# Requeuing the transfers of pre-summed weights and the next chunk's tokens in a gated WKV + FFN block, and moving chunk 0's low parts of activations from GpSimd to VectorE

## The chip, the cores and the metric

The kernel runs on one core of a Trainium2 chip. The metric is the device time of one execution in microseconds (us). The engines are TensorE (PE, matmuls; PEld is its weight load), VectorE (DVE), ScalarE (ACT) and GpSimd (POOL). SyncE (SP) computes nothing here: it waits on semaphores and issues most DMAs, so its program is called the SP queue below. POOL issues the DMAs that add while they copy.

## The reference, cut to what matters

```python
# x, ctx: (16, 256, 512) float32
x = x + tanh(g_xattn) * wkv(time_decay, time_first, k=layernorm(x), v=ctx)   # a scan over the 256 tokens
h = silu(layernorm(x) @ W1.T) * (layernorm(x) @ W3.T)                        # 512 -> 2048
x = x + tanh(g_ffn) * (fwht(h) @ W2.T)                                       # Hadamard transform, 2048 -> 512
```

## The kernel before

The 4096 tokens are cut into 8 chunks of 512 tokens (two batches each). The Hadamard transform is folded into W2 at the start. Each float32 matmul operand is split into a float16 high part and a bfloat16 low part, and three matmuls (high by high, high by low, low by high) replace one.

**Weights.** W1 and W3 come in 16 units (two units make a piece of 256 hidden channels, so there are 8 pieces). `unit_hi` (ACT) and `unit_lo` (DVE) split a unit in place; the semaphore `raw_lo` counts the units that are ready. `put_plain(p)` on SP stores a finished piece to the DRAM scratch `up_stage`, for use by the later chunks.

**Sums.** Chunks 1 to 7 use a block scheme with fewer products, which needs sums of weight blocks. POOL forms these in DRAM (`up_sums`) for four groups of two pieces, each in four steps of two DMAs: `copy_group`, then the accumulating DMAs `add_first`, `add_second` and `add_third`. Before each step POOL waits until the step before it of the same group has landed. `load_again(n)` on SP brings the sums of unit n into one of three buffers, after `add_third` of its group has landed and (from n = 3 on) after buffer n - 3 was used. `weight_parts(n)` on DVE splits them (lines 1451 and 1454) into one of two output buffers, and `put_sums(n)` on SP stores that to `up_stage`. `weight_parts(n)` waits for the load, and from n = 2 on also for the store `put_sums(n - 2)`. `load_pair` fetches one piece, plain and sums, for the block scheme.

**Stages.** Run 0 and Run 1 are the two halves of chunk 0. After a preamble, `ffn(Run(1))` works through 16 hidden tiles j. For each tile PE makes a gate product (`pg`), a linear product (`pl`), and the down product of tile j - 2; ACT takes the silu of the gate (L964), DVE multiplies (`times_lin`, L1398) and rounds to float16 (`hidden_hi`, L1405), and POOL subtracts the high part from the product (`hidden_lo`, L1683). Between those, in an order written out by hand in `FIRST_AT`, the engines prepare chunk 1 (called Run 2 in the code): token moments `tok`, scans `scan_b` and `scan_a` (L1267) with a scaling of each on ACT (L899), `over`, the residual, the mean and the variance (PE matmuls L607 and L612 in PE's own order), normalising. `next_tok` takes the token moments of the chunk after that (Run 3), whose tokens `load_tokens(2)` brings into `bv` (L1211 reads them). `unit_slot` says at which tile ACT and DVE split the units 8 to 15, and `SUMS_AT` at which tile DVE does which `weight_parts`. From `pairs(Run(2))` on, chunks 1 to 7 go through the block scheme in eight pairs of tiles each (lines 714 to 737).

**Order.** Every engine and the SP queue work in program order; semaphores tie them. PE must have all 16 units (`raw_lo` 16) before tile 14. In the preamble POOL also clamps 16 tiles of W2 (`tile_clamp`, L1688); PE's `less_hi(i)` (L636) waits for the clamp of tile i.

```python
def hidden_lo(run, j):                       # on POOL
    pool.wait_ge(hid_hi, run.tile(j))
    pool.tensor_tensor(hl[...], hf[...], hh[...], ALU.subtract).then_inc(hid_lo, 1)
...
def load_x(c):                               # on SP; load_tokens(c) follows it with no wait of its own
    sp.wait_ge(x1_done, c * NB)
```

Of the kernel before, what the change touches and what calls it, by code (L numbers as in the profile page):

```python
# [21 lines left out]
SLOTS = H // P  # L22
# [39 lines left out]
                num=8, inv=8, over=9, resid=9, mean=(11, 1), centre=10, square=11,  # L62
                sum_var=11, var=(13, 0), rsqrt=13, norm=14, next_tok=11)

SUMS_AT = {4: (0,), 5: (1,), 7: (2,), 8: (3,), 10: (4,), 11: (5,), 12: (6,), 13: (7,)}
LATE_SUMS = {0: (8,), 1: (9,), 2: (10,), 3: (11,), 4: (12, 13), 5: (14, 15)}
# [3 lines left out]
GROUPS = ((0, 2), (2, 4), (4, 6), (6, 8))  # L70

STEPS_AT = {0: ((0, "second"),), 1: ((1, "first"),), 2: ((0, "third"),), 3: ((2, "copy"),), 4: ((1, "second"),),
            5: ((1, "third"),), 6: ((2, "first"),), 7: ((3, "copy"),), 8: ((2, "second"),), 9: ((2, "third"),),
            10: ((3, "first"),), 11: ((3, "second"),), 12: ((3, "third"),)}


def flamingo_block(nc, xt_in, x_in, v_in, w1_in, w3_in, w2_in, mats_in, stage, up_sums, factor_rows, out):
    with ExitStack() as ctx:
# [224 lines left out]

        unit_slot = {0: (8, 9), 1: (10, 11), 3: (12,), 4: (13,), 12: (14, 15)}
        places = (0, 1, 2, 3, 4, 5, 0, 1, 6, 7, 8, 9, 10, 11, 12, 13)
# [66 lines left out]
        def _(sp):  # L372
# [39 lines left out]
            def put_plain(p):  # L412

                sp.wait_ge(raw_lo, 2 * p + 2)
                sp.dma_start(stage[p][:, 0, :], piece(p)).then_inc(plain_put[p], 16)
# [101 lines left out]
            load_unit(15)  # L517
            put_plain(3)
            for n in range(0, 3):
                load_again(n)  # L520
            put_plain(4)
            put_plain(5)
            put_sums(0)
            load_again(3)
            put_sums(1)
            put_plain(6)
            load_again(4)
            put_sums(2)
            load_again(5)
            put_sums(3)  # L530
            load_again(6)
            load_v(2)
            put_sums(4)
            load_again(7)
            load_x(2)
            load_tokens(2)
            put_sums(5)
            put_plain(7)
            put_factors(Run(3))
# [639 lines left out]
        def _(dve):  # L1179
# [228 lines left out]
            def hidden_tile(run, j):  # L1408
                times_lin(run, j)
                hidden_hi(run, j)  # L1410

            def channel_sum(run, which):

# [43 lines left out]
            def ffn(run):  # L1457

                ahead = Run(2, 1)
                for j in range(SLOTS):  # L1460
# [18 lines left out]
                    if j == SLOTS - 1:  # L1479
                        plain_lo(ahead, 0)  # L1480
                        sums_lo(ahead, 0)
                    hidden_tile(run, j)
                    if at(j, "resid"):
                        residual(ahead, 0)
                        residual(ahead, 1)
                        channel_sum(ahead, 0)
# [172 lines left out]
        def _(pool):  # L1659
# [70 lines left out]
            def ffn():  # L1730

                for j in range(SLOTS):
                    hidden_lo(Run(1), j)
                    for g, step in STEPS_AT.get(j, ()):
                        if step == "copy":
                            copy_group(g)
                        if step == "first":
                            add_first(g)
                        if step == "second":
                            add_second(g)  # L1740
                        if step == "third":
                            add_third(g)

# [27 lines left out]
            copy_group(0)  # L1771
            for i in range(3, 11):
                tile_clamp(i)
            pool.wait_ge(rows_mm, 2 * KT)
            for j in range(0, 2):
                hidden_lo(Run(0), j)
            add_first(0)
            copy_group(1)
            for i in range(11, 13):
# [3 lines left out]
            for i in range(13, TILES):  # L1783
                tile_clamp(i)
            ffn()
            pairs(Run(2, 1, 0))
# [54 lines left out]
```

## Time and profile before

| | |
|---|---|
| median of 3 runs | 1056.58 us (1054.04 to 1057.97) |
| the profiled execution | 1057.62 us, of which the span of its instructions is 1055.8 us |
| PE busy | 997.6 us, 94% of the span |
| DVE busy | 801.8 us, 76% |
| ACT, POOL busy | 439.6 us, 274.2 us |
| mean granted TensorE clock | 0.988 of full speed |

The profiled execution lies 1.0 us above the median. Its span is what the traces below are measured in. PE is busy for nearly all of it, so time is lost where PE has gaps or runs at the lower clock level, and the chain that ended last runs on PE for 69% of the span.

### The profile page before, as it was taken

The numbers are of one execution on the slowest core, as the hardware profiler recorded it, in microseconds if no ns is written. First come the engines' busy times: TensorE is split into PE (matmuls) and PEld (weight loads), VectorE is DVE, ScalarE is ACT, GpSimd is POOL, SyncE is SP. The second block draws the span as 40 slices with busy tenths as digits, with TensorE's granted clock in tenths as the row PEclk, the third lists the DMA queues.
The fourth block names the chain that finished last, engine by engine and source line by source line (L and its number), as shares of the span: only waits on it lengthen the run. The fifth ranks groups of instructions, "written<-read, shape, count | busy, mean of one in ns | idle before, by whom it ended". The sixth has DMA issues, their size and how long they took to land.

```text
span 1055.8 us, 17503 instructions
## 1 busy us (share of the span) xinstructions
PE 997.6 (94%) x6988; PEld 691.6 (66%) x6988; DVE 801.8 (76%) x1288; ACT 439.6 (42%) x736; POOL 274.2 (26%) x212
## 2 busy tenths in 40 slices
PE   5799899689999999999999999999999999999998
PEld 4565344256677677776777777777777777777775
DVE  7977594989989995889769995889669994753334
ACT  6875342246243443455243542444243542522221
POOL 1344232211432033211422124221322124211111
PEclk9999999799999999999999999999999999999999
DMA  9699999694885446354745446353645433444331
GB/s 352 233 340 291 321 255 227 109 355 168 293 301 173 151 188 240 100 213 155 267 164 178 146 177 239 114 218 143 264 160 180 163 126 151 160 166 165 125 145 41
DMA packets 47042, 210.03 MB, mean 199 GB/s; under 512 B 9328, under 2 KB 26864, under 8 KB 36336
## 3 DMA queue, kind: packets, MB, share of 16 engines
q1 hardware_dynamic: 38128, 192.13, 50.2%
q0 software_dynamic: 8832, 16.78, 7.6%
q8 instruction: 55, 0.90, 0.3%
q14 instruction: 27, 0.22, 0.1%
HBM read 183.70 MB, written 41.97 MB: 214 GB/s over the span
## 4 chain that ended last, share of the span: by engine, by line
PE 69%; DVE 17%; DMA 6%; issue 5%; ACT 2%; SPq 0%; DVEq 0%; POOL 0%
PE pl L714 8%; PE pl L716 8%; PE pl L715 8%; PE po L726 7%; PE po L728 7%; PE pg L714 6%; PE pg L715 6%; PE pg L716 6%; PE po L737 4%; PE po L735 4%; DMA bv<-x_tok 2%; DMA wts<-up_stage 2%; DVE x L1432 2%; DVE work L1604 2%; DVE bv L1295 1%
## 5 line engine op out<-in xcount | busy, mean ns | idle before, releaser
L1759 POOL TENSOR_TENSOR work<-work 128x512 bf16<-128x512 f32 x112 | 163.9, 1464 | 595.4 <-DVE work L1604 595.4
L726 PE MATMUL po<-work,w 128*128 128x512 f16 x456 | 173.0, 379 | 2.2 <-DVE x L1432 1.3
L728 PE MATMUL po<-work,w 128*128 128x512 f16 x456 | 172.8, 379 | 0.0
L1060 ACT ACTIVATE work<-work 128x256 f32<-128x256 f32 x168 | 68.4, 415 | 210.2 <-DVE work L1511 210.1
L714 PE MATMUL pg<-wts 128*128 128x256 f16 x448 | 122.5, 273 | 4.8 <-DVE work L1511 4.7
L1511 DVE TENSOR_TENSOR work<-pl,wts 128x256 f32<-128x256 f32 x168 | 65.1, 414 | 80.1 <-PE pl L716 77.5
L715 PE MATMUL pg<-wts 128*128 128x256 bf16 x448 | 122.4, 273 | 0.0
L716 PE MATMUL pg<-wts 128*128 128x256 f16 x448 | 122.4, 273 | 0.0
L714 PE MATMUL pl<-xn,wts 128*128 128x256 f16 x448 | 122.3, 273 | 0.0
L715 PE MATMUL pl<-xn,wts 128*128 128x256 bf16 x448 | 122.2, 273 | 0.0
L716 PE MATMUL pl<-xn,wts 128*128 128x256 f16 x448 | 122.1, 273 | 0.0
L716 PE MATMUL pl<-wts 128*128 128x256 f16 x448 | 122.1, 273 | 0.0
L715 PE MATMUL pl<-wts 128*128 128x256 bf16 x448 | 122.1, 273 | 0.0
L714 PE MATMUL pl<-wts 128*128 128x256 f16 x448 | 122.1, 273 | 0.0
L1604 DVE TENSOR_SCALAR work<-work 128x512 f16<-128x512 f32 x112 | 91.3, 815 | 8.2 <-PE po L737 0.5
L735 PE MATMUL po<-work,w 128*128 128x512 bf16 x228 | 86.4, 379 | 0.0
L737 PE MATMUL po<-work,w 128*128 128x512 bf16 x228 | 86.4, 379 | 0.0
L1034 ACT COPY wts<-pg 128x512 f32<-128x512 f32 x56 | 32.6, 582 | 123.9 <-PE pg L716 123.9
L726 PEld LDWEIGHTS po<-work,w 128*128 128x128 f16 x456 | 44.6, 98 | 52.7 <-DVE x L1432 9.6
L728 PEld LDWEIGHTS po<-work,w 128*128 128x128 bf16 x456 | 44.6, 98 | 39.4
L714 PE MATMUL pg<-xn,wts 128*128 128x256 f16 x224 | 61.3, 274 | 4.9 <-DMA wts<-up_stage 3.6
L1511 DVE TENSOR_TENSOR work<-pg,early 128x256 f32<-128x256 f32 x56 | 23.6, 421 | 55.6 <-PE pg L716 54.8
(206 smaller groups left out, 2159.6 us busy)
## 6 DMA issues: line engine op xcount, KB each, us to landing
wts<-up_stage SPq DMA_DIRECT2D x56, 2048.0 KB, 8.0
up_stage<-wts SPq DMA_DIRECT2D x8, 1024.0 KB, 13.2
up_stage<-wts SPq DMA_DIRECT2D x16, 512.0 KB, 8.2
ev<-ctx_t SPq DMA_DIRECT2D x7, 1024.0 KB, 11.0
xin<-x_t SPq DMA_DIRECT2D x7, 1024.0 KB, 7.5
bv<-x_tok SPq DMA_DIRECT2D x7, 1024.0 KB, 10.0
out_t<-x SPq DMA_DIRECT2D x7, 1024.0 KB, 4.8
wts<-up_sums SPq DMA_DIRECT2D x11, 512.0 KB, 9.0
```

Source lines behind the costliest of these rows:

```text
L714: pe.matmul(bank, hi, ah, start=(start and k == 0), stop=False, skip_group_check=True)
L715: pe.matmul(bank, hi, al, start=False, stop=False, skip_group_check=True)
L716: mm = pe.matmul(bank, lo, ah, start=False, stop=(stop and k == 1), skip_group_check=True)
L726: pe.matmul(po[:, d, :], w2h[:, j, d * P:d * P + P], hh[:, b, :], start=start, stop=False, skip_group_check=True)
L728: pe.matmul(po[:, d, :], w2l[:, j, d * P:d * P + P], hh[:, b, :], start=False, stop=False, skip_group_check=True)
L735: pe.matmul(po[:, d, :], w2h[:, j + 1, d * P:d * P + P], hl[:, b + 1, :], start=False, stop=False, skip_group_check=True)
L737: pe.matmul(po[:, d, :], w2h[:, j, d * P:d * P + P], hl[:, b, :], start=False, stop=((p - 1) % PAIRS == PAIRS - 1), skip_group_check=True) ...
L1034: act.copy(early1[:, w, :], chain_fifth[w]).then_inc(kept1, 1)
L1060: act.activation(sg[:, slot, cols], src, ACT.Silu, scale=(1.0, -1.0)[slot]).then_inc(acted, 1)
L1511: dve.tensor_tensor((sg, hf)[w][:, slot, b * T:b * T + T], bank, other, ALU.add).then_inc(joined, 1)
L1604: dve.tensor_scalar(hh[:, 2 * (p % 2) + slot, :], hf[:, slot, :], F16_MAX, -F16_MAX, ALU.min, ALU.max).then_inc(pair_hi, 1)
L1759: pool.tensor_tensor(hl[:, b, :], hf[:, slot, :], hh[:, b, :], ALU.subtract).then_inc(pair_lo, 1)
```

## The change

`add_first(0)`, `copy_group(1)`, `add_second(0)`, `add_first(1)` and `add_third(0)` are issued earlier in POOL's preamble, and POOL's part of `ffn` is only the remaining DMA steps, with no `hidden_lo` between them. `hidden_lo` of Run 1's sixteen tiles is done by DVE right behind `hidden_hi`. Units 14 and 15 are split at tiles 4 and 5 (they were split at 12), `next_tok` goes from tile 11 to 12, the `weight_parts` are placed anew, and the SP queue is reordered.

```diff
-                sum_var=11, var=(13, 0), rsqrt=13, norm=14, next_tok=11)
-SUMS_AT = {4: (0,), 5: (1,), 7: (2,), 8: (3,), 10: (4,), 11: (5,), 12: (6,), 13: (7,)}
+                sum_var=11, var=(13, 0), rsqrt=13, norm=14, next_tok=12)
+SUMS_AT = {5: (0, 1), 8: (2,), 10: (3, 4), 11: (5,), 13: (6,), 14: (7,)}
...
-        unit_slot = {0: (8, 9), 1: (10, 11), 3: (12,), 4: (13,), 12: (14, 15)}
+        unit_slot = {0: (8, 9), 1: (10, 11), 3: (12,), 4: (13, 14), 5: (15,)}
...
             put_plain(3)
+            put_plain(4)
+            put_plain(5)
             for n in range(0, 3):
                 load_again(n)
-            put_plain(4)
-            put_plain(5)
+            put_plain(6)
             put_sums(0)
             load_again(3)
             put_sums(1)
-            put_plain(6)
             load_again(4)
+            put_plain(7)
+            load_v(2)
             put_sums(2)
             load_again(5)
+            load_x(2)
+            load_tokens(2)
             put_sums(3)
             load_again(6)
-            load_v(2)
             put_sums(4)
             load_again(7)
-            load_x(2)
-            load_tokens(2)
             put_sums(5)
-            put_plain(7)
...
+            def hidden_lo(run, j):                 # on DVE
+                if j == 0:
+                    dve.wait_ge(hid_lo, Run(0).tile(AHEAD - 1))
+                if j >= HBUF:
+                    dve.wait_ge(down, run.down(j - HBUF))
+                dve.wait_ge(hid_hi, run.tile(j))
+                dve.tensor_tensor(hl[...], hf[...], hh[...], ALU.subtract).then_inc(hid_lo, 1)
...
             def ffn():                             # on POOL
-                for j in range(SLOTS):
-                    hidden_lo(Run(1), j)
-                    for g, step in STEPS_AT.get(j, ()): ...
+                add_second(1)
+                for g in range(2, len(GROUPS)):
+                    copy_group(g)
+                    add_third(g - 1)
+                    add_first(g)
+                    add_second(g)
+                add_third(len(GROUPS) - 1)
```

DVE's order from tile 4's product on, before (L1438 and L1441 split a unit, L1451 and L1454 are a `weight_parts`):

```order
L1398 TENSOR_TENSOR work<-work,pl 128x512
L1405 TENSOR_SCALAR work<-work 128x512
L1438 TENSOR_SCALAR wts<-wts 128x1024
L1441 TENSOR_TENSOR wts<-x,wts 128x1024
L1451 TENSOR_SCALAR wts<-wts 128x1024
L1454 TENSOR_TENSOR wts<-wts 128x1024
L1398 TENSOR_TENSOR work<-work,pl 128x512
L1405 TENSOR_SCALAR work<-work 128x512
L1451 TENSOR_SCALAR wts<-wts 128x1024
L1454 TENSOR_TENSOR wts<-wts 128x1024
```

The same stretch of DVE in the changed kernel (L1394, L1401 and L1415 are the product, its high part and its low part; L1444 and L1447 a unit, L1457 and L1460 a `weight_parts`):

```order
L1394 TENSOR_TENSOR work<-work,pl 128x512
L1401 TENSOR_SCALAR work<-work 128x512
L1415 TENSOR_TENSOR work<-work 128x512
L1444 TENSOR_SCALAR wts<-wts 128x1024
L1447 TENSOR_TENSOR wts<-x,wts 128x1024
L1444 TENSOR_SCALAR wts<-wts 128x1024
L1447 TENSOR_TENSOR wts<-xn,wts 128x1024
L1394 TENSOR_TENSOR work<-work,pl 128x512
L1401 TENSOR_SCALAR work<-work 128x512
L1415 TENSOR_TENSOR work<-work 128x512
L1444 TENSOR_SCALAR wts<-wts 128x1024
L1447 TENSOR_TENSOR wts<-xn,wts 128x1024
```

The low part is new behind each high part; units 14 and 15 (the rows that read `xn`) now stand at tiles 4 and 5, ahead of the first two `weight_parts`, which both follow at tile 5.

POOL's preamble before, from its fourth W2 clamp on (L1711 is `add_first`, L1700 `copy_group`, L1683 `hidden_lo`, L1688 a clamp, L1720 `add_second`):

```order
L1688 TENSOR_SCALAR w<-w 128x4x128 [waits w2_hi] x8
L1683 TENSOR_TENSOR work<-work 128x256 [waits hid_hi,rows_mm]
L1683 TENSOR_TENSOR work<-work 128x256 [waits hid_hi]
L1711 DMA up_sums<-w_t 512x1x256 [waits summed0_0]
L1711 DMA up_sums<-w_t 512x1x256 [waits summed0_1]
L1700 DMA up_sums<-w_t 16x16384 x2
L1688 TENSOR_SCALAR w<-w 128x4x128 [waits w2_hi] x2
```

The same place in the changed kernel (L1718 is `add_first`, L1707 `copy_group`, L1695 a clamp, L1690 `hidden_lo`, L1727 `add_second`):

```order
L1695 TENSOR_SCALAR w<-w 128x4x128 [waits w2_hi] x5
L1718 DMA up_sums<-w_t 512x1x256 [waits summed0_0]
L1718 DMA up_sums<-w_t 512x1x256 [waits summed0_1]
L1707 DMA up_sums<-w_t 16x16384 x2
L1695 TENSOR_SCALAR w<-w 128x4x128 [waits w2_hi] x3
...
L1727 DMA up_sums<-up_sums 256x256 [waits summed0_0]
L1727 DMA up_sums<-up_sums 256x256 [waits summed0_1]
L1718 DMA up_sums<-w_t 512x1x256 [waits summed1_0]
L1718 DMA up_sums<-w_t 512x1x256 [waits summed1_1]
L1695 TENSOR_SCALAR w<-w 128x4x128 [waits w2_hi] x2
```

The clamps of W2's tiles 11 and 12 (the last row of each) now stand behind two steps that wait for DMAs to land, `add_second(0)` and `add_first(1)`.

## Rows read from the trace of the kernel before

**Rows 1.** The page, busy time of each engine over the span.

```profile
PE 997.6 (94%) x6988; PEld 691.6 (66%) x6988; DVE 801.8 (76%) x1288; ACT 439.6 (42%) x736; POOL 274.2 (26%) x212
```

**Rows 2.** Busy time by stretch: stretch, length, PE, PEld, DVE, ACT, POOL, PEclk, DMA share, GB/s.

```profile
125.90:131.20 5.30, 0.12 (x1) 0.02 (x1) 3.61 (x4) 3.16 (x6) 1.95 (x3) 0.91 1.01 311
131.20:139.20 8.00, 7.99 (x24) 3.01 (x25) 7.86 (x7) 4.86 (x5) 2.35 (x3) 0.64 1.02 176
139.20:147.10 7.90, 7.90 (x37) 3.45 (x36) 7.76 (x6) 7.74 (x8) 4.34 (x6) 1.00 0.84 270
195.20:212.50 17.30, 17.29 (x72) 7.34 (x72) 16.75 (x20) 8.56 (x10) 2.62 (x2) 0.91 1.06 176
400.00:1055.80 655.80, 647.19 (x4783) 467.28 (x4780) 466.96 (x778) 250.66 (x446) 161.92 (x110) 1.00 0.46 168
```

**Rows 3.** Waits of PE from 73 to 217 us: total, times, longest.

```profile
PE pg L645 <- DVE wts L1441: 12.5, 1, 12.5
PE pg L645 <- ACT work L964: 6.1, 2, 5.2
PE pg L714 <- DMA wts<-up_stage: 3.6, 1, 3.6
```

**Rows 4.** DVE in order of time, 90 to 216 us: start, duration, instruction, idle time before.

```profile
98.84 0.69 DVE L1398 TENSOR_TENSOR work<-work,pl 128x512 f32<-128x512 f32 x1 [3.11 <-PE pl L647]
...
115.32 0.69 DVE L1451 TENSOR_SCALAR wts<-wts 128x1024 f16<-128x1024 f32 x1 [12.83 <-DMA wts<-up_sums]
116.05 1.23 DVE L1454 TENSOR_TENSOR wts<-wts 128x1024 bf16<-128x1024 f32 x1
...
119.04 2.06 DVE L1454 TENSOR_TENSOR wts<-wts 128x1024 bf16<-128x1024 f32 x1
...
121.22 2.37 DVE L1254 TENSOR_TENSOR ev<-ev 128x1028 f32<-128x1028 f32 x2
123.51 4.48 DVE L1267 TENSOR_TENSOR_SCAN eb<-decays,ev 128x1028 f32<-128x1028 f32 x2
...
163.73 2.35 DVE L1337 TENSOR_TENSOR eb<-x,pst 128x1024 f32<-128x1024 f32 x2 [2.15 <-PE pst L607]
...
184.71 2.47 DVE L1211 BATCH_NORM_STATS2 parts<-bv 128x6 f32<-128x512 f32 x4 [11.07 <-DMA bv<-x_tok]
...
212.62 0.68 DVE L1398 TENSOR_TENSOR work<-work,pl 128x512 f32<-128x512 f32 x1
```

**Rows 5.** One group of DVE's high parts, 78.8 to 213.4 us: busy, mean ns.

```profile
L1405 DVE TENSOR_SCALAR work<-work 128x512 f16<-128x512 f32 x11 | 4.7, 427 | 1.2
```

**Rows 6.** PE in order of time: a `less_hi`, and the end of tile 5's linear product.

```profile
69.96 0.38 PE L636 MATMUL po<-w,minus 128*128 128x512 f16 x1
...
107.29 0.38 PE L653 MATMUL po<-work,w 128*128 128x512 f16 x1
```

**Rows 7.** ACT in order of time: the scaling behind `scan_b`.

```profile
128.03 2.56 ACT L899 ACTIVATE ev<-ev,cc 128x512 f32<-128x512 f32 x4 [14.33 <-DVE eb L1267]
```

**Rows 8.** The SP queue in order of time: when it issued its DMAs.

```profile
106.31 2.59 SPq L426 DMA_DIRECT2D wts<-up_sums  x2
...
169.55 0.61 SPq L406 DMA_DIRECT2D bv<-x_tok  x1
...
196.22 0.97 SPq L447 DMA_DIRECT2D wts<-up_stage  x1
```

**Rows 9.** POOL in order of time: `add_first(0)`, clamps 11 and 12, `add_third(0)`, a `hidden_lo`.

```profile
59.43 2.75 POOL L1711 DMA_DIRECT2D up_sums<-w_t  x2
...
67.85 1.32 POOL L1688 TENSOR_SCALAR w<-w 128x512 f16<-128x512 f16 x2 [4.65 <-ACT w L983]
...
93.94 0.87 POOL L1727 DMA_DIRECT2D up_sums<-up_sums  x1
...
118.55 1.47 POOL L1683 TENSOR_TENSOR work<-work 128x512 bf16<-128x512 f32 x1 [14.08 <-DVE work L1405]
```

**Rows 10.** Issue to landing: POOL's four DMAs of 59 to 61.5 us; `put_sums(3)`.

```profile
DMA to landing us min/median/max: 13.0/19.4/23.4
...
up_stage<-wts SPq DMA_DIRECT2D x1, 512.0 KB, 7.9
```

More of the change, by code:

```diff
@@ L70 @@
 GROUPS = ((0, 2), (2, 4), (4, 6), (6, 8))
-STEPS_AT = {0: ((0, "second"),), 1: ((1, "first"),), 2: ((0, "third"),), 3: ((2, "copy"),), 4: ((1, "second"),),
-            5: ((1, "third"),), 6: ((2, "first"),), 7: ((3, "copy"),), 8: ((2, "second"),), 9: ((2, "third"),),
-            10: ((3, "first"),), 11: ((3, "second"),), 12: ((3, "third"),)}
 def flamingo_block(nc, xt_in, x_in, v_in, w1_in, w3_in, w2_in, mats_in, stage, up_sums, factor_rows, out):
@@ L1410, in hidden_tile @@
                 hidden_hi(run, j)
+            def hidden_lo(run, j):
[4 more added lines that the diff above has]
+                dve.wait_ge(hid_hi, run.tile(j))
+                dve.tensor_tensor(hl[:, j % HBUF, run.cols(j)], hf[:, j % 2, run.cols(j)],
+                                  hh[:, j % HBUF, run.cols(j)], ALU.subtract).then_inc(hid_lo, 1)
             def channel_sum(run, which):
@@ L1482, in ffn @@
                     hidden_tile(run, j)
+                    hidden_lo(run, j)
                     if at(j, "resid"):
@@ L1730, in ffn @@
             def ffn():
-                for j in range(SLOTS):
-                    hidden_lo(Run(1), j)
[L1734 to L1742, printed above, removed]
+                add_second(1)
[5 more added lines that the diff above has]
+                add_third(len(GROUPS) - 1)
             def pairs(run, front=True):
@@ L1771, in _ @@
             copy_group(0)
-            for i in range(3, 11):
+            for i in range(3, 8):
+                tile_clamp(i)
+            add_first(0)
+            copy_group(1)
+            for i in range(8, 11):
                 tile_clamp(i)
@@ L1776, in _ @@
                 hidden_lo(Run(0), j)
-            add_first(0)
-            copy_group(1)
+            add_second(0)
+            add_first(1)
             for i in range(11, 13):
@@ L1784, in _ @@
                 tile_clamp(i)
+            add_third(0)
             ffn()
```

## The prediction

> **What bounds the kernel now.** First the page: PE is busy 94% of the span [rows 1]. Then busy time by stretch: from 400 us to the end PE works 647.2 of 655.8 us at full clock [rows 2], and the change touches nothing there. So the gain or loss must come from the first 220 us, the part in which chunk 0 runs and the weights are prepared. There I read the waits of PE [rows 3]: 12.5 us for the last unit of W1/W3 ahead of tile 14, 5.2 us for one silu ahead of tile 8 (the 6.1 us of the row is this one and a short one), 3.6 us for the first `load_pair`. The stretches show what a gap costs beside itself: after the 5.2 us gap the clock is 0.64 for 8 us, in which PE does 24 matmuls; at full clock it does 37 in 7.9 us, so 24 take 5.1 us and 2.9 us are lost to the 1.2 GHz level. After the 12.5 us gap the 72 matmuls of 195.2 to 212.5 take 17.3 us where they should take 15.4, so 1.9 us are lost [rows 2]. PE's recoverable time is 5.2 + 2.9 + 12.5 + 1.9 = 22.5 us; the 3.6 us gap stands apart.
>
> Third, what is late behind those waits, on DVE [rows 4]. DVE sat idle 12.8 us until 115.3 for the first sums, because `load_again(0)` was issued at 106.3 [rows 8], after `add_third(0)`, which POOL issued at 93.9 behind a `hidden_lo` [rows 9]. Everything behind it in DVE's order slid: `scan_b` started at 123.5, ACT's scaling waited for it until 128.0 [rows 7], the silu of tile 7 stands behind that on ACT, and PE needed it. Later DVE idled 11.1 us until 184.7 for chunk 2's tokens, issued at 169.55 [rows 4, 8], and the units 14 and 15 stood behind that wait.
>
> **The change part by part.** I walk DVE's order, the queue that decides, and check PE against it.
>
> Low parts on DVE. A 128x512 operation of two inputs takes 0.69 us, the high part 0.43 us [rows 4, 5]. The trace has no such subtraction on DVE. Bounds: 0.43 from below; from above 1.23, the cost of twice the elements [rows 4]. I take 0.7, the same shape and kind. Twelve full tiles and four half ones add 12 x 0.7 + 4 x 0.4 = 10 us. Against it stands a saving. `weight_parts` L1454 takes 1.23 us alone, but 2.06 at 119.04, while POOL's `hidden_lo` ran from 118.55 [rows 4, 9]. I count nine such DVE operations beside a `hidden_lo`, so 9 x 0.83 = 7.5 us go away. Net cost some 2.5 us over the stage; without the saving 10 us, with the low bound below zero.
> The Trainium skill, "SBUF — State Buffer", section "Who interferes with whom", says that a DVE instruction with two SBUF inputs contends with a GpSimd instruction that reads SBUF, and that the later one blocks wholly. By that rule the 119.04 one waits until 118.55 + 1.47 = 120.02 and ends at 121.25, 2.21 us; the row says 2.06. The rule would put the saving at up to 9 x 0.98 = 8.8 us and the net at 1.2 us; nothing below uses that.
>
> First sums. POOL can issue `add_third(0)` once clamps and `add_second(0)` are through, which I put at 77 to 81 us, not 93.9: `add_second(0)` now goes out near 63 and lands some 14 us later. The load goes out 12.4 us behind (106.3 - 93.9), at 90 to 94, and lands 9 us behind that (115.3 - 106.3), plus up to 3 us for the two plain stores now ahead of it: 102 to 106. DVE: tile 4 at 98.8 as before, + 1.8 for product, high and low part, + 2 x 1.65 for units 13 and 14 (each 0.42 + 1.23) = 103.9. Tile 5's linear product ends near 107.4 [rows 6]; + 1.9 and unit 15 gives 111.0, and only there are the sums wanted, so no wait. Two `weight_parts` at 1.9: 114.7. Weighing 2.4 and scan 4.5 end at 121.6; before, 128.0. `scan_b` is 6.4 us earlier, and the silu of tile 7 comes at 124.6 + 0.6, before PE wants it (125.9). PE's first gap and its clock loss, 8.1 us, go. The silu of tile 8, behind ACT's second scaling, only gains 6.4 us: PE waits about 1.6 us there instead. PE at the mean's matmul is 8.1 - 1.6 = 6.5 us earlier.
>
> Tiles 7 to 11. `weight_parts(3)` leaves tile 8 for tile 10, so DVE reaches its wait for the mean 7 us earlier and still waits: mean at 163.7 - 6.5 = 157.2. From there before took 9.9 us to the end of the second channel sum (163.7 to 184.7 - 11.1 = 173.6). Now `weight_parts(3)` adds 1.9, a low part 0.7, less 0.8 of POOL's disturbance: 157.2 + 11.7 = 168.9.
> A new wait stands in it. `weight_parts(5)` needs the store `put_sums(3)`, which cannot go out before `weight_parts(3)` at 161.5, four us before it is wanted (165.3). Before, that store had been out since tile 8. With its 7.9 us [rows 10] it lands at 169.4: 4 us of waiting, end at 173. Bounds: nothing if it lands in 3.8 us; 11 us if it takes the 15.1 us that the tokens took (184.7 - 169.55), since they are queued just ahead of it. Behind the wait stand the channel sum, PE's variance matmul and so the linear product of tile 13: PE loses some 3 us there.
>
> Tiles 12 to 15. The tokens are issued behind the residual at 151.5 and land by 167, wanted at 175: the 11.1 us wait goes. Units 14 and 15 are long done, so the 12.5 us gap and its 1.9 us go. DVE from the start of the token moments to the end of tile 15's product took 213.3 - 184.7 = 28.6 us. Less tile 12's product (1.1) and the two units (4.0), less 1.5 of disturbance, plus two low parts 1.4, plus 0.7 for the reciprocal root on ACT: 24.1. So 173 + 1.9 (tile 12) + 24.1 = 199. The block scheme cannot start before tile 15's product. PE itself would be through tile 13's down product at 212.5 - 22.5 + 1.6 + 3 to 5 = 195 to 197. DVE is the bound, at 199; the wait there replaces the 3.6 us one. `load_pair(0)` goes out at 181 (before 196.2, landing 19.8 us later), so it lands at 201 at the worst, 192 when less is queued.
>
> W2's clamps. Clamps 11 and 12 ran at 67.85, and `less_hi(11)` at 69.96 [rows 6, 9], a slack of 1.4 us. They now stand behind `add_first(1)`, which waits for `copy_group(1)`. POOL issues `add_first(0)` and that copy at 46 to 51 instead of 59.4. Then they took 13.0 to 23.4 us [rows 10], and from 59.4 the last was in at 84.7. The same from 46.2 gives 71.5, the clamp at 73.5 and 4.3 us of delay for PE; with the low end 13 us after 51, nothing. I take 2 us. This delay moves everything behind it.
>
> Sum: the block scheme starts at 199 + 2 = 201 instead of 216.1. Gain 15 us, on the span 1055.8 - 15 = 1041. The profiled run is 1.0 above the median, so 1056.6 - 15 = **1041.5 us**. Chunk 1's remaining work keeps its distance to PE: DVE ends its preparation 2.8 us behind PE's start, where before it began `scale` 2.5 us behind.
>
> **The rivals.**
> 1. *Better than that (0.16).* The store is quick and the copy lands in time: 4 + 2 us more, gain 21, 1035.5 us. For it: DMA engines are less loaded once the plain stores are early. Against it: tokens and `load_x(2)` are 2 MB just ahead of the store.
> 2. *DVE's new chain eats more (0.18).* The sums or the store land late (11 us instead of 4), or the low part costs 1.2 us. Gain 3 to 9, 1048 to 1053. For it: DVE is busy nearly throughout from 110 to 170 us.
> 3. *Slower (0.06).* POOL now waits for its DMAs with PE's clamps behind. Lost is every microsecond by which `copy_group(1)` lands after 67, and it decides from a landing at 67 + 17 = 84 us, 34 us after issue, against 23.4 as the longest seen. At 40 us it would be 1063.
> A page rule bears on this one: the Trainium skill, same page, "A bandwidth-pool intuition that's wrong", says that POOL's DMAs wait for descriptors while DVE runs some two-port operations. By that rule the chain on POOL would be late by DVE operations of 0.4 to 1.2 us each (an estimate from rows), not by tens; I see DMA issues of 2.75 us for two [rows 9] and give it no more weight.
> 4. *No change (0.05).* The gaps only move to the end of the stage.
>
> **How the numbers follow.** The forecast (gain 10 to 18, 1038.5 to 1046.5) has 0.55. The 80% range takes in rival 1 and most of rival 2: 1034 to 1052. A measurement of this kernel can tell about 0.5%, 5.3 us, from no change. Faster: 0.55 + 0.16 + two thirds of rival 2 = 0.84; slower 0.05; same 0.11.
>
> **What would show it.** Right: DVE's 12.8 and 11.1 us waits gone; PE's 12.5 us wait for L1441 gone; L1454 at 1.23 us throughout; block scheme starting near 201. The new waits to look for: `weight_parts(5)` for an `up_stage` store, PE for the variance's channel sum, PE ahead of `less_hi(11)` for a POOL clamp, PE at pair 0 for DVE. Wrong if the first sums still land after 111, or if PE stands still before 74 us.

## The result, and the profile after

| | before | changed |
|---|---|---|
| median | 1056.58 us (1054.04 to 1059.15, 9 runs) | 1049.68 us (1047.17 to 1052.58, 9 runs) |
| ratio | | 0.9937, 95% interval 0.9921 to 0.9952 |
| the profiled execution: span | 1055.8 us | 1047.9 us |
| start of the block scheme | 216.1 us | 206.9 us |

The changed kernel is 6.9 us faster. I had forecast 15. It was measured once more among the experiments below, again beside the kernel before: 9.7 us faster, ratio 0.9904 [0.9887, 0.992]. The two intervals just miss each other, so differences of 0.3% between ratios that were taken apart say little below.

The page of the changed kernel, busy time:

```profile
PE 992.5 (95%) x6922; PEld 692.4 (66%) x6988; DVE 802.5 (77%) x1304; ACT 439.9 (42%) x736; POOL 254.5 (24%) x196
```

PE's work is what it was (some of its records are missing here, 6922 of 6988), so the difference is again one of gaps and of the clock. In the numbering of the changed kernel `less_hi` is L632, the gate product L641, the silu L960, `times_lin` L1394, `hidden_lo` L1415, `weight_parts` L1457 and L1460, the clamp L1695, `add_first` L1718, `copy_group` L1707, `add_second` L1727, `add_third` L1734 and the block scheme starts at L710.

Waits of PE after, from 40 to 330 us: total, times, longest.

```profile
PE po L632 <- POOL w L1695: 9.5, 1, 9.5
PE pg L641 <- ACT work L960: 3.8, 4, 1.9
PE pg L710 <- DVE work L1394: 3.4, 1, 3.4
```

Against [rows 3]: the 12.5 us wait for the units is gone, the waits for the silu are short ones, and the wait at the block scheme is for DVE instead of for `load_pair`. All that was forecast. The first line was forecast too, but at 2 us: PE stands still 9.5 us for a clamp of W2, nearly as long as what was removed (6.9 us when the changed kernel was profiled again).

PE in order of time, and the stretch behind that gap (PE, PEld, DVE, ACT, POOL, PEclk, DMA share, GB/s):

```profile
79.78 0.61 PE L632 MATMUL po<-w,minus 128*128 128x512 f16 x1 [9.47 <-POOL w L1695]
...
206.93 0.37 PE L710 MATMUL pg<-xn,wts 128*128 128x256 f16 x1 [3.44 <-DVE work L1394]
```

```profile
79.00:84.30 5.30, 4.52 (x15) 3.17 (x16) 1.38 (x2) 2.83 (x5) 2.60 (x6) 0.65 1.17 257
```

The `less_hi` that ran at 69.96 [rows 6] now runs at 79.78, and behind the gap the granted clock is 0.65, the 1.2 GHz level for most of the stretch. POOL tells why, in order of time:

```profile
46.28 2.83 POOL L1718 DMA_DIRECT2D up_sums<-w_t  x2
47.62 2.51 POOL L1707 DMA_DIRECT2D up_sums<-w_t  x2
...
62.06 0.92 POOL L1727 DMA_DIRECT2D up_sums<-up_sums  x1 [2.40 <-DMA up_sums<-w_t]
72.14 0.91 POOL L1727 DMA_DIRECT2D up_sums<-up_sums  x1 [9.15 <-DMA up_sums<-w_t]
74.73 1.30 POOL L1718 DMA_DIRECT2D up_sums<-w_t  x1 [1.69 <-DMA up_sums<-w_t]
77.76 1.30 POOL L1718 DMA_DIRECT2D up_sums<-w_t  x1 [1.73 <-DMA up_sums<-w_t]
78.42 1.87 POOL L1695 TENSOR_SCALAR w<-w 128x512 f16<-128x512 f16 x2
...
86.51 1.87 POOL L1734 DMA_DIRECT2D up_sums<-up_sums  x2
```

Issue to landing of the two `add_first(0)` DMAs of 46.3 and 47.0 us:

```profile
DMA to landing us min/median/max: 15.5/20.2/24.9
```

Clamps 11 and 12 ran at 67.85 before [rows 9] and run at 78.42 now. Ahead of them in POOL's order stand `add_second(0)`, which waits for `add_first(0)` to land, and `add_first(1)`, which waits for `copy_group(1)`. The second DMA of `add_first(0)` took 24.9 us, to 71.9. The two copies, issued at 47.6 and 48.1, took 26.8 and 29.3 us, to 74.4 and 77.4, and held the next two issues until 74.7 and 77.8. The landing of the last copy is thus what the clamps were waiting for in the end.

DVE after, in order of time, answering to [rows 4]:

```profile
110.38 0.69 DVE L1394 TENSOR_TENSOR work<-work,pl 128x512 f32<-128x512 f32 x1 [2.43 <-PE pl L643]
111.70 0.69 DVE L1415 TENSOR_TENSOR work<-work 128x512 bf16<-128x512 f32 x1
...
122.55 0.69 DVE L1457 TENSOR_SCALAR wts<-wts 128x1024 f16<-128x1024 f32 x1
123.27 1.23 DVE L1460 TENSOR_TENSOR wts<-wts 128x1024 bf16<-128x1024 f32 x1
...
128.77 4.48 DVE L1263 TENSOR_TENSOR_SCAN eb<-decays,ev 128x1028 f32<-128x1028 f32 x2
...
169.00 2.35 DVE L1333 TENSOR_TENSOR eb<-x,pst 128x1024 f32<-128x1024 f32 x2 [2.52 <-PE pst L603]
...
176.92 0.69 DVE L1457 TENSOR_SCALAR wts<-spare 128x1024 f16<-128x1024 f32 x1
...
182.58 2.46 DVE L1207 BATCH_NORM_STATS2 parts<-bv 128x6 f32<-128x512 f32 x4
...
206.09 0.68 DVE L1394 TENSOR_TENSOR work<-work,pl 128x512 f32<-128x512 f32 x1
```

The reader is to see two things. The waits of 12.8 us for the sums and 11.1 us for the tokens are gone: `weight_parts(0)` at 122.55 and the token moments at 182.58 start with no wait. And DVE is late before it begins: tile 4's product is at 110.38, not at 98.84. So the first scan is at 128.77, later than the 123.51 of before, and still the stage ends earlier. The low part takes 0.69 us, as taken. The SP queue after, and the landing of `put_sums(3)`, the store of 173.24:

```profile
99.37 0.37 SPq L422 DMA_DIRECT2D wts<-up_sums  x1
...
162.90 0.55 SPq L402 DMA_DIRECT2D bv<-x_tok  x1
...
173.24 0.33 SPq L428 DMA_DIRECT2D up_stage<-wts  x1
...
188.47 0.39 SPq L443 DMA_DIRECT2D wts<-up_stage  x1
```

```profile
up_stage<-wts SPq DMA_DIRECT2D x1, 512.0 KB, 3.2
```

### The profile page after: what moved, and what is told of

The parts are those of the page before. It is cut to its first block, busy times and chain, and to the rows that moved or that the text cites. A ratio compares the mean times of both kernels' runs of the same rounds, so it can differ in the third digit from the quotient of the medians.

```text
span 1047.9 us, 17438 instructions
## 1 busy us (share of the span) xinstructions
PE 992.5 (95%) x6922; PEld 692.4 (66%) x6988; DVE 802.5 (77%) x1304; ACT 439.9 (42%) x736; POOL 254.5 (24%) x196
## 4 chain that ended last, share of the span: by engine, by line
PE 67%; DVE 19%; issue 6%; ACT 3%; DMA 3%; POOL 0%; DVEq 0%; ACTq 0%
PE pl L712 8%; PE pl L710 8%; PE pl L711 8%; PE po L722 7%; PE po L724 7%; PE pg L710 6%; PE pg L712 6%; PE pg L711 6%; PE po L733 4%; PE po L731 3%; DMA up_sums<-w_t 3%; DVE x L1438 2%; DVE work L1611 2%; DVE bv L1291 1%; DVE eb L1287 1%
## 5 line engine op out<-in xcount | busy, mean ns | idle before, releaser
L710 PE MATMUL pg<-wts 128*128 128x256 f16 x448 | 122.5, 273 | 4.9 <-DVE work L1518 4.9
L710 PE MATMUL pl<-xn,wts 128*128 128x256 f16 x448 | 122.4, 273 | 0.0
L710 PE MATMUL pl<-wts 128*128 128x256 f16 x448 | 122.4, 273 | 0.0
L733 PE MATMUL po<-work,w 128*128 128x512 bf16 x228 | 86.4, 379 | 2.9
L710 PE MATMUL pg<-xn,wts 128*128 128x256 f16 x224 | 61.3, 274 | 4.8 <-DVE work L1394 3.4
L731 PE MATMUL po<-work,w 128*128 128x512 bf16 x172 | 65.2, 379 | 0.0
```

Source lines behind the costliest of these rows:

```text
L710: pe.matmul(bank, hi, ah, start=(start and k == 0), stop=False, skip_group_check=True)
L731: pe.matmul(po[:, d, :], w2h[:, j + 1, d * P:d * P + P], hl[:, b + 1, :], start=False, stop=False, skip_group_check=True)
L733: pe.matmul(po[:, d, :], w2h[:, j, d * P:d * P + P], hl[:, b, :], start=False, stop=((p - 1) % PAIRS == PAIRS - 1), skip_group_check=True) ...
```

## The experiments

The theory: the gain that is missing is the time for which POOL's waits for its own DMAs hold back the clamps. The rivals: removing that only uncovers the next late thing, the first sums; or DVE, with the low parts, takes longer than I counted. Each kernel has its own profile, and is timed against the kernel before on the same chip. Ratios are to the kernel before, with 95% intervals. "Block start" is the first L710 (or L714) matmul in the profiled execution. Kernels that start from the kernel before have its line numbers, but for the low parts alone.

**Clamps first.** In the changed kernel, the clamps go ahead of what waits for landings.

```diff
-            add_second(0)
-            add_first(1)
             for i in range(11, 13):
                 tile_clamp(i)
...
             for i in range(13, TILES):
                 tile_clamp(i)
+            add_second(0)
+            add_first(1)
             add_third(0)
```

> The changed kernel, with all of POOL's W2 clamps and its hidden_lo of Run 0 put ahead of add_second(0) and add_first(1); add_first(0) and copy_group(1) stay early. Theory A (the forecast fell short because PE stood still 9.5 us ahead of less_hi(11) for a POOL clamp behind a DMA wait, and lost some 2 us of clock after it): less_hi(11) back at 70 us, tile 4's product on DVE at 99 instead of 110.4, block scheme starting at 196 to 198 instead of 207, time 1049.7 - 10 = 1039.5 us, ratio to before 0.984. Theory B (the first sums then become the bound, since add_second(0) goes out at 75 and the sums land at 112 to 118): a wait of 3 to 7 us on DVE ahead of the first weight_parts, time 1042 to 1046.

Measured: 1046.46 us, ratio 0.9893 [0.9877, 0.9909], block start 204.28. DVE in order of time:

```profile
100.89 0.69 DVE L1394 TENSOR_TENSOR work<-work,pl 128x512 f32<-128x512 f32 x1 [4.12 <-PE pl L643]
...
118.81 0.80 DVE L1457 TENSOR_SCALAR wts<-wts 128x1024 f16<-128x1024 f32 x1 [5.62 <-DMA wts<-up_sums]
```

PE's 9.5 us wait is gone and DVE is 9.5 us earlier at tile 4 (100.89 for 110.38). Of that only 2.7 us are left at the block start. 5.6 us go into a new wait for the first sums: in POOL's new order `add_second(0)` goes out at 75.2, `add_third(0)` at 86.1 and 90.2 and the load of the sums at 106.6. So the first rival holds too, as the next thing in line. Theory B had this wait (3 to 7 us), theory A's block start of 196 to 198 did not come, and the time lies 0.5 us above B's. The two intervals, this one and the changed kernel's 0.9904 [0.9887, 0.992], overlap, so this kernel is not shown to be faster than the changed one; that the clamps' place costs what PE waits is shown by the traces here and by the pair at tile 6 below.

**The POOL order of before in the preamble.** In the changed kernel, `add_first(0)` and `copy_group(1)` go back to where they were, then the clamps, then the later steps.

```diff
-            add_first(0)
-            copy_group(1)
             for i in range(8, 11):
...
-            add_second(0)
-            add_first(1)
+            add_first(0)
+            copy_group(1)
             for i in range(11, 13):
...
+            add_second(0)
+            add_first(1)
             add_third(0)
```

> The changed kernel with POOL's preamble in the order of before: add_first(0) and copy_group(1) at 59.4 us, clamps ahead of add_second(0). Theory A: less_hi(11) at 70 us, and what the early add_first(0) brings is only whether the first sums are in time; here add_second(0) goes out near 78 us, the sums land near 115, 4 us after DVE wants them, time 1041 to 1044. Theory B predicts the same wait as in the kernel with clamps first, so no difference between the two; theory A with early sums in time predicts 2 to 4 us between them.

Measured: 1050.59 us, ratio 0.9935 [0.9921, 0.995], block start 207.12. No wait for a clamp, and of DVE:

```profile
DVE wts L1457 <- DMA wts<-up_sums: 8.2, 1, 8.2
```

The sums are wanted at tile 5 and come 8.2 us late. The time is that of the changed kernel, by another wait: the early issue of `add_first(0)` bought nothing that its waits did not take back. Against the kernel with clamps first, which keeps the early issue, it is 4 us slower (the intervals 0.9877 to 0.9909 and 0.9921 to 0.995 are apart): theory A's 2 to 4 us between the two, not theory B's nothing.

**Only the POOL preamble of the change**, in the kernel before.

```diff
-STEPS_AT = {0: ((0, "second"),), 1: ((1, "first"),), 2: ((0, "third"),), 3: ((2, "copy"),), 4: ((1, "second"),),
+STEPS_AT = {3: ((2, "copy"),), 4: ((1, "second"),),
...
+            add_first(0)
+            copy_group(1)
+            for i in range(8, 11):
...
+            add_second(0)
+            add_first(1)
             for i in range(11, 13):
...
+            add_third(0)
             ffn()
```

> The kernel before with only POOL's preamble of the changed kernel (early add_first(0), copy_group(1), add_second(0), add_first(1), add_third(0)); everything else as before. Theory A (the clamp wait costs what it costs whatever else is done): PE waits 9.5 us ahead of less_hi(11), tile 4's product 11 us later at 110; but DVE's 12.8 us wait for the first sums shrinks by the same, since they are loaded at 99 and not 106, so scan_b comes at 123 to 124 as before and the time is within 3 us of before, 1054 to 1059. Theory B' (delays add up whatever waits stand behind them): 11 us slower than before, 1067.

Measured: 1056.82 us, ratio 0.9989 [0.9977, 1.0002]. Waits of PE:

```profile
PE pg L645 <- DVE wts L1441: 10.9, 1, 10.9
PE po L636 <- POOL w L1688: 9.5, 1, 9.5
```

The wait for the clamp comes with the preamble alone, and is of the same 9.5 us. Tile 4's product is at 110.30, the first scan at 125.28, and theory B', that the delays add up to 1067 us, falls. The load of the sums went out at 97.7 and DVE no longer waited for them (12.8 us before). The kernel lost PE's 9.5 us and its clock ahead of tile 4 and got back what the late sums had cost behind it.

**Only the low parts on DVE**, in the kernel before, with the steps of POOL as they were but no `hidden_lo` between them.

```diff
+            def hidden_lo(run, j):
...
+                dve.tensor_tensor(hl[:, j % HBUF, run.cols(j)], hf[:, j % 2, run.cols(j)],
+                                  hh[:, j % HBUF, run.cols(j)], ALU.subtract).then_inc(hid_lo, 1)
...
                     hidden_tile(run, j)
+                    hidden_lo(run, j)
...
             def ffn():
                 for j in range(SLOTS):
-                    hidden_lo(Run(1), j)
```

> The kernel before with only the low parts of Run 1 on DVE; POOL runs through its DMA steps in their old order with nothing between, behind all clamps. Forecast's step: low parts cost DVE 0.69 us each for full tiles and L1454 falls from up to 2.06 to 1.23 us. add_third(0) goes out near 88 instead of 93.9, so the first sums land 3 to 5 us earlier; the later waits (units 14 and 15 behind the tokens at tile 11) stay. Ratio to before 0.995 to 1.000. If low parts were a real burden on DVE (theory E), 1.003 to 1.008.

Measured: 1056.93 us, ratio 0.9989 [0.9976, 1.0002]. Waits of DVE (L1461 is `weight_parts` here):

```profile
DVE wts L1461 <- DMA wts<-up_sums: 10.7, 1, 10.7
DVE parts L1211 <- DMA bv<-x_tok: 9.0, 1, 9.0
```

By itself the move to DVE costs nothing and brings nothing: the added work lies in the idle time that [rows 4] show, which shrinks from 12.8 and 11.1 to 10.7 and 9.0. I had also expected the first sums 3 to 5 us earlier; their load went out at 107.1, against 106.3 before. (This profile is 1.0 us later from the preamble on.) The second rival finds no support here, but this kernel has idle time to hide it in; where DVE is the bound the part on the prediction tests it.

**Only the queues and tables**, in the kernel before: `unit_slot`, `SUMS_AT`, `next_tok` and the SP order of the change; POOL's program as before, low parts included.

```diff
-                sum_var=11, var=(13, 0), rsqrt=13, norm=14, next_tok=11)
+                sum_var=11, var=(13, 0), rsqrt=13, norm=14, next_tok=12)
-SUMS_AT = {4: (0,), 5: (1,), 7: (2,), 8: (3,), 10: (4,), 11: (5,), 12: (6,), 13: (7,)}
+SUMS_AT = {5: (0, 1), 8: (2,), 10: (3, 4), 11: (5,), 13: (6,), 14: (7,)}
...
-        unit_slot = {0: (8, 9), 1: (10, 11), 3: (12,), 4: (13,), 12: (14, 15)}
+        unit_slot = {0: (8, 9), 1: (10, 11), 3: (12,), 4: (13, 14), 5: (15,)}
```

> The kernel before with only the SP queue's new order and the new tiles of units 14 and 15, weight_parts and next_tok; low parts stay on POOL and POOL's DMA steps where they were. Theory A (the recovered 12.5 us and 5.2 us gaps come from these places alone): first sums land at 115 as before and are wanted at 111, so a wait of 4 us stays; PE's 12.5 us gap for the last unit goes; block scheme starts at 197 to 201, time 1038 to 1042, better than the changed kernel. Theory C (without free-running POOL steps the later sums are late, and POOL's interference with DVE stays): time 1045 to 1050.

Measured: 1048.89 us, ratio 0.9916 [0.99, 0.9932], block start 207.24. Waits of DVE, and of PE:

```profile
DVE wts L1451 <- DMA wts<-up_sums: 7.7, 1, 7.7
DVE wts L1451 <- DMA up_stage<-wts: 5.1, 1, 5.1
PE pst L612 <- DVE psum L1427: 3.4, 1, 3.4
```

The gain of the whole change is in this part, which alone does as well as all of it. Here, too, stand the two waits that I had forecast behind the moved `weight_parts(3)`: 5.1 us for the store, and 3.4 us of PE for the channel sum behind it. Theory A's 1038 to 1042 us did not come; the time lies in theory C's range.

**Clamps first, and the first two `weight_parts` at tile 6.** The kernel of the first experiment with the sums wanted one tile later.

```diff
-SUMS_AT = {5: (0, 1), 8: (2,), 10: (3, 4), 11: (5,), 13: (6,), 14: (7,)}
+SUMS_AT = {6: (0, 1), 8: (2,), 10: (3, 4), 11: (5,), 13: (6,), 14: (7,)}
```

> The kernel with POOL's clamps first, and the first two weight_parts moved from tile 5 to tile 6, behind scan_b and tile 6's product, so DVE wants the first sums at 122 us and not at 113. Theory B (with the clamps freed, the landing of the first sums at 118.8 is the bound, 5.6 us of DVE's idle time): no DVE wait for sums, scan_b starts at 116 instead of 125, block scheme at 198 to 200 instead of 204.3, time 5 us below the kernel with clamps first, ratio to before 0.984. Theory D (the store that weight_parts(5) waits for takes the place of it): a DVE wait of 3 to 5 us for an up_stage store, and 1 to 3 us gained.

Measured: 1042.2 us, ratio 0.9836 [0.9816, 0.9856]. PE at the block start, DVE's longest wait but for the linear products, and DVE at the mean:

```profile
198.49 0.27 PE L710 MATMUL pg<-xn,wts 128*128 128x256 f16 x1 [2.59 <-DVE work L1394]
```

```profile
DVE wts L1457 <- DMA up_stage<-wts: 3.0, 1, 3.0
```

```profile
157.49 2.35 DVE L1333 TENSOR_TENSOR eb<-x,pst 128x1024 f32<-128x1024 f32 x2 [2.53 <-PE pst L603]
```

With both waits out of the way DVE runs as the prediction walked it without a delay by the clamps: mean at 157.5 (worked out: 157.2), block start at 198.5 (worked out: 199). The time is near the 1041.5 us that I had forecast for the change (16 us below the 1058.24 of the kernel before beside it), but it takes two edits that the change does not have.

**The sums at tile 6 in the other orders of POOL.** The same line of `SUMS_AT` in the queues-only kernel:

> The kernel before with the new SP queue and places (low parts and POOL's order as before), and the first two weight_parts at tile 6. Theory B: the 7.7 us wait for the first sums goes, as landing at 121 meets a demand at 122; the 5.1 us wait for the store of sums 3 stays or grows to 8 (theory D); block scheme at 200 to 203 instead of 207.2, ratio to before 0.985 to 0.989. Against the kernel with clamps first and sums at tile 6 it tells what low parts on DVE and free-running POOL steps are worth: my walk says the low parts cost DVE 2.5 us net.

in the kernel with POOL's preamble of before:

> The kernel with clamps first and the first sums at tile 6, with add_first(0) and copy_group(1) back at 59.4 us. Theory G (the early issue of these two is worth nothing once the sums are wanted at 120.7): the first sums land at 120 to 123, DVE waits 0 to 2 us, ratio 0.983 to 0.986. If the early issue matters, DVE waits 4 us or more and the ratio is 0.988.

and in the changed kernel itself, with the changed kernel as it is beside it:

> The changed kernel with nothing altered but the first two weight_parts at tile 6. Theory A (the changed kernel loses its time ahead of less_hi(11), and its first sums are in time anyway): DVE never waited for the sums there, so PE's 9.5 us wait and the block scheme's start near 207 stay, scan_b alone comes 3.7 us earlier; 0 to 3 us better than the changed kernel. If the 16 us of the kernel with clamps first and sums at tile 6 came from the sums' place (theory H), it is 5 us or more better.

> The changed kernel once more, beside its variants on one chip: ratio to before 0.992 to 0.995, PE's 9 to 10 us wait ahead of less_hi(11), block scheme at 207.

| order of POOL, low parts on | sums at tile 5 | sums at tile 6 |
|---|---|---|
| as before, POOL | 1048.89, 0.9916 [0.99, 0.9932] | 1048.61, 0.9898 [0.9872, 0.9924] |
| preamble as before, DVE | 1050.59, 0.9935 [0.9921, 0.995] | 1043.52, 0.9855 [0.9835, 0.9874] |
| clamps first, DVE | 1046.46, 0.9893 [0.9877, 0.9909] | 1042.2, 0.9836 [0.9816, 0.9856] |
| the change, DVE | 1048.99, 0.9904 [0.9887, 0.992] | 1049.19, 0.9907 [0.9891, 0.9923] |

(The kernels were timed on three chips, so compare the ratios. The change's row is from one chip.) In the two middle rows, where the sums came late, tile 6 brings 0.8% and 0.6%. In the changed kernel they were not late, and it brings nothing. In the first row the wait for the sums goes too, but another takes its place, and the 0.985 to 0.989 and the block start of 200 to 203 that I expected there did not come (210.21). Theory G holds by its ratio: in the right column the early issue of `add_first(0)` is worth nothing clear of noise. The repeat of the changed kernel missed two of its numbers, the wait ahead of `less_hi(11)` (6.9 us, not 9 to 10) and the ratio, and met the block start (206.73).

The last two rows of the right column differ by the place of the clamps alone: block start 198.49 and 207.62. The second profile is 1.3 us later from the preamble on (POOL's last clamp ahead of `add_first(0)` is at 46.88, against 45.62), so some 8 of these 9 us are the clamps' place, and 0.7% in the ratios. This is its cleanest price. On one chip, the second row's 1043.52 and the last row's 1049.19 say the same in sign; they differ by the issue of `add_first(0)` as well.

The changed kernel with the sums at 6, waits of PE:

```profile
PE po L632 <- POOL w L1695: 7.0, 1, 7.0
```

The queues-only kernel with the sums at 6, waits of PE and DVE:

```profile
PE po L653 <- POOL work L1683: 11.6, 1, 11.6
...
DVE work L1398 <- POOL work L1683: 6.5, 1, 6.5
```

Here a `hidden_lo` on POOL is stuck behind a wait for a landing, and PE behind it for 11.6 us. `add_third(1)` went out at 123.4 and 128.4, each when a DMA of `add_second(1)` had landed, and the low part ran only then, at 128.99. So the low parts on DVE can be worth something after all, once the sums' wait no longer hides it: they take PE's operands off the engine that waits for DMAs. How much is not shown. The right column has 1048.61 against 1043.52, but the intervals touch, the six runs of the first spread over 8.6 us (1043.23 to 1051.78) with the profiled one near the top (1051.48), and POOL's later steps are placed differently in the two as well.

**One landing ahead of the clamps.** The changed kernel with `copy_group(1)` behind `add_second(0)` and `add_first(1)` behind `add_third(0)`, so that the clamps wait for `add_first(0)` alone, and this has no copy beside it.

```diff
             add_first(0)
-            copy_group(1)
...
             add_second(0)
-            add_first(1)
+            copy_group(1)
...
             add_third(0)
+            add_first(1)
```

> The changed kernel with copy_group(1) not early but behind add_second(0), and add_first(1) behind add_third(0), so that only add_second(0)'s wait for add_first(0) stands ahead of clamps 11 and 12. If add_first(0) landed 24.9 us after issue because POOL's own copy shared the engines with it (theory Q), it now lands at 13 to 15 us, near 61, PE waits 0 to 1 us ahead of less_hi(11), and tile 4's product is at 101; the time is then set by the first sums. If the load of SP's transfers alone makes it slow (theory L), it still lands near 70, PE waits 4 to 6 us there, time like the changed kernel or up to 3 us better.

Measured: 1042.63 us, ratio 0.9845 [0.9827, 0.9864], block start 202.53. POOL in order of time, the landing of its first two DMAs, and the wait of PE:

```profile
46.08 2.83 POOL L1718 DMA_DIRECT2D up_sums<-w_t  x2
...
62.67 0.90 POOL L1727 DMA_DIRECT2D up_sums<-up_sums  x1 [3.20 <-DMA up_sums<-w_t]
70.15 0.89 POOL L1727 DMA_DIRECT2D up_sums<-up_sums  x1 [6.58 <-DMA up_sums<-w_t]
```

```profile
DMA to landing us min/median/max: 16.3/19.7/23.1
```

```profile
PE po L632 <- POOL w L1695: 2.7, 1, 2.7
```

The landing hardly changes without the copies: 23.1 us, where the seven other profiles with the early issue have 20.6 to 24.9. So the copies beside it are not what makes it long; what does is open (below). Theory L had the landing right, but neither the wait (4 to 6 us) nor the time (at most 3 us better). The wait for the clamp falls from 9.5 (6.9 in the repeat) to 2.7 us. That is what the landing of `add_first(0)` alone costs PE. The rest was the later landing, that of the copies ahead of `add_first(1)`.

This kernel, at 0.9845, is also better than clamps first with the sums at tile 5 (0.9893). It has `add_second(0)` out early, so the load of the first sums goes out at 92.3, they land at 106.5, and DVE doesn't wait for them.

**`weight_parts(5)` at tile 12**, on top of clamps first and sums at 6.

```diff
-SUMS_AT = {6: (0, 1), 8: (2,), 10: (3, 4), 11: (5,), 13: (6,), 14: (7,)}
+SUMS_AT = {6: (0, 1), 8: (2,), 10: (3, 4), 12: (5,), 13: (6,), 14: (7,)}
```

> The kernel with clamps first and the first sums at tile 6, and weight_parts(5) moved from tile 11 to tile 12. Theory D (the store of sums 3 is what delays weight_parts(5), and through the channel sum PE's variance matmul): DVE's 3.0 us wait for an up_stage store and PE's 2.0 us wait for psum go, block scheme at 195 to 196.5 instead of 198.5, 2 to 3 us better, ratio to before 0.981. If DVE's total work is the bound there (theory F), only the order of waits changes and the time stays within 1 us.

Measured: 1039.66 us, ratio 0.9819 [0.9805, 0.9834]. PE and DVE in order of time:

```profile
196.98 0.27 PE L710 MATMUL pg<-xn,wts 128*128 128x256 f16 x1 [3.46 <-DVE work L1394]
```

```profile
170.74 0.69 DVE L1457 TENSOR_SCALAR wts<-spare 128x1024 f16<-128x1024 f32 x1
```

The wait for the store (3.0 us) is gone and the block start 1.5 us earlier, although this profile, too, is 1.3 us later from the preamble on. In the medians the two intervals overlap, so this last step is read from the trace, not from the time. It is the fastest of the kernels measured, 19 us below the kernel before on its chip (1058.71).

## Why the prediction was off by 8 us

The sum had 15 us and the result is 6.9. By its steps:

- **First sums: right in effect, in part by luck.** DVE did not wait for them. But their load went out at 99.4 (105.0 in the repeat), not at 90 to 94, and landed at 109.7 and, for the second unit, 116.5 (the first at 116.6 in the repeat), not at 102 to 106. The walk wants them at 111.0 and 112.9; DVE was 11.5 us late by then and reached them at 122.55. I had `add_second(0)` go out "near 63"; its second DMA went out at 72.1, and `add_third(0)` at 86.5, not at 77 to 81. With one landing ahead of the clamps the step came out nearly as written: load at 92.3, landed at 106.5, no wait. With clamps first it cost 5.6 us.
- **Low parts on DVE: right.** 0.69 us each, and `weight_parts` at 1.23 us wherever it ran up to 214 us (it was 2.06 beside POOL's `hidden_lo` [rows 4]). The saving that was set against the added work is there. The net shows in the kernel with clamps first and sums at 6, where the mean is at 157.5 for 157.2 and the block start at 198.5 for 199: the low parts did not cost DVE more than counted. The walk left out the four half tiles ahead of tile 4; with the clamps first and sums at 6, tile 4 was at 99.46, 0.6 us behind [rows 4].
- **Units and tokens: right.** The 12.5 us and 11.1 us waits are gone.
- **The store ahead of `weight_parts(5)`: 4 us taken, nothing in the changed kernel.** The store landed in 3.2 us, at 176.4, and was wanted at 176.92. The wait itself is real: 5.1 and 4.2 us in the two queues-only kernels, 0.6 to 3.0 us in the six variants of the changed kernel that keep `weight_parts(5)` at tile 11, 0.6 when the changed kernel was profiled again. My value lay inside that scatter, and the range's low bound (nothing) is what came.
- **W2's clamps: this is the step that failed.** I took 2 us, with 4.3 as the upper bound. With the clamps in their new place tile 4 is at 110.38 against 99.46 with the clamps first and the sums at 6: 10.9 us, of them 9.5 of waiting and the rest mostly the clock of 0.65 behind it. (On one chip, between the repeat and the kernel with clamps first, sums at 6 and `weight_parts(5)` at 12, it is 109.36 - 100.56 = 8.8 us.) The mechanism is the one of rival 3, and it was written down in the sum, only too small; by that rival's own count, every microsecond after 67, the copy that landed at 77.4 costs 10.4. The error is the landing time. I carried the landings of 59.4 over to 46.3, and there the later of the copies took 29.3 us, not 23.4, and landed at 77.4, where my latest was 71.5; and of the 0 to 4.3 us that this gave I took 2. I also left out that `add_second(0)` waits for `add_first(0)` ahead of the same clamps. That alone costs PE 2.7 us, as the kernel with one landing shows, but in the changed kernel the later landing covers it.
- **From the block start on.** The prediction has this part unchanged. It took 841.0 us against 839.7. Over all thirteen profiles besides that of before it lies between 838.4 and 841.0: 838.4 to 839.5 in the three others with chunk 0's low parts on POOL, 838.8 to 841.0 in the ten with them on DVE. The two ranges overlap, but their means (with the kernel before in the first) are 839.1 and 840.4. So the 1.3 us is more likely an effect of low parts on DVE, or of what goes with them, than scatter; no run settles it, and the prediction put it at nothing.

The number, 1049.7, lies in the range of rival 2 (1048 to 1053), but not for its reason: DVE's own chain took no longer than counted. Of the signs of being wrong that I had named, "PE stands still before 74 us" came (it stopped at 70.3); "the first sums land after 111" did not for the first unit (109.7) and did in the repeat (116.6). Two slips in the working change nothing: [rows 6] put the end of tile 5's linear product at 107.7 and not 107.4, and the chances of "faster" add up to 0.83.

The corrected sum: 15 - (10.9 - 2) for the clamps - 0.6 for the half tiles + 4 for the store is 9.5 at the block start, measured 216.1 - 206.9 = 9.2. Less the 1.3 behind it that is the 7.9 of the spans. The profiled execution of before lay 1.0 above its median and that of the changed kernel on it (1049.68), which leaves 6.9.

Open is why the early DMAs land so late. The second one of `add_first(0)` took 20.6 to 24.9 us in the eight profiles that issue it at 46 to 48 us, and 17.9 to 19.4 us in the six that issue it at 60 to 61 us. Without the copies beside them it still took 23.1 us. The load of the DMA engines is hardly different: their mean busy share is 1.06 over 46 to 72 us in the changed kernel and 0.99 over 59 to 85 us before, at 323 and 318 GB/s. No kernel took the SP queue's transfers of that time away, and none varied what DVE does while POOL issues, the subject of the second paragraph of rival 3.

## What to carry to other kernels

On an engine that works in program order, a wait for a transfer's landing delays everything queued behind it: before issuing a step earlier, list each wait between its new place and the next thing another engine needs, and take the latest landing among them, since the transfers run side by side, with a landing time that has a margin over that of the old place. Here five clamps of W2 above instead of below two such steps were worth some 8 us.

When an early wait is removed, the whole chain behind it moves up and the next transfer becomes the late one; so try edits in pairs. From the changed kernel (0.9904 and 0.9937), clamps first alone gave 0.9893 and the sums at tile 6 alone 0.9907, but the two together 0.9836.

## What the hardware showed that I had not expected

- The two accumulating DMAs of `add_first(0)` took 13.0 and 18.2 us when issued at 59.4 and 60.1 us, and 15.5 and 24.9 us when issued at 46.3 and 47.0; the two copies behind them took 20.7 and 23.4, and 26.8 and 29.3 us. Two DMAs that were issued 0.7 us apart landed 10 us apart.
- A stop of some 2 us of PE ahead of tile 4 (for a token statistic on ACT) cost clock in one kernel and not in another. With the clamps first, after 2.03 us of idling, the granted clock was 0.77 and 0.81 in the next stretches; in the same order with sums at 6, after 2.11 us, it stayed at 1.00. The product of tile 4 came 1.4 us later in the first. Of the six profiles with clamps ahead of the waits and low parts on DVE, which stop there for 1.95 to 2.46 us, two stay at 1.00 and four fall. Windows of the first kernel, then of the second:

```profile
95.00:99.00 4.00, 3.08 (x12) 1.49 (x13) 1.74 (x3) 3.98 (x6) 0.00 (x0) 0.77 1.09 338
99.00:103.00 4.00, 4.00 (x16) 1.69 (x15) 1.90 (x4) 1.22 (x2) 0.87 (x1) 0.81 1.20 204
```

```profile
95.00:99.00 4.00, 2.83 (x15) 1.56 (x16) 1.99 (x3) 3.98 (x6) 0.00 (x0) 1.00 1.08 332
```

The two kernels have the same program on PE up to there, so such a difference between two profiles is no effect of an edit.
